# Layer-norm scales taken ahead of the last tile, routing mixed with hidden products, and a second cross attention written out with its last steps one tile later

## The reference

```python
x = x + L0_xattn(layernorm(x), ctx)      # 16 heads
x = x + L0_attn(layernorm(x))            # state space: gates, decays
x = x + L0_ffn(layernorm(x))             # 16 blocks, the best 4 of each row
x = x + L1_xattn(layernorm(x), ctx)      # one head
x = x + L1_attn(layernorm(x))            # causal self attention
x = x + L1_ffn(layernorm(x))             # 4-bit weights, quantized activations
```

## Time and profile before

| what | value |
|---|---|
| median of 3 runs | 1695.85 us (1692.62 to 1696.95) |
| the profiled execution | 1692.85 us, span of its instructions 1691.1 us |
| PE busy | 1557.8 us, 92% of the span |
| DVE / ACT / POOL busy | 1180.3 / 888.4 / 723.6 us |
| mean granted PE clock | 0.969 of full |
| PE busy, 850 to 990 us | 122.38 of 140.00, clock 0.98 |
| PE busy, 990 to 1211 us | 211.32 of 221.00, clock 0.93 |
| PE busy, 1248 to 1386 us | 124.24 of 138.00, clock 0.99 |
| PE busy, 1386 to 1442 us | 51.94 of 56.00, clock 0.97 |
| PE busy, 1442 to 1691 us | 199.20 of 249.10, clock 0.91 |

### The profile page before, as it was taken

One profiled execution on the slowest core, in us unless ns is written; L12 is line 12 of the kernel. 1 busy time (PEld: TensorE's weight loads), 2 busy tenths in 40 slices (PEclk: granted clock), 3 DMA queues, 4 the chain that ended last, 5 costly groups with the idle time before them and its releaser, 6 DMA issues. The chain is left out here.

```text
span 1691.1 us, 33888 instructions
## 1 busy us (share of the span) xinstructions
PE 1557.8 (92%) x13881; PEld 815.0 (48%) x13990; DVE 1180.3 (70%) x1952; ACT 888.4 (53%) x1189; POOL 723.6 (43%) x348
## 2 busy tenths in 40 slices
PE   6999999999999999999888989999889989799469
PEld 3445555555555555555444564344534444444124
DVE  6588888888888888887557458998622233526981
ACT  1487777777777777777463224431212222326650
POOL 1478888888787888886306813320000000000000
PEclk9999999999999999999999979999899999999779
DMA  4489999999999999999925653569779934000001
GB/s 140 128 182 192 190 192 194 186 198 188 194 193 198 195 182 198 191 190 171 185 70 156 225 226 79 143 175 209 233 311 398 393 143 188 1 1 0 1 0 50
DMA packets 555526, 282.73 MB, mean 167 GB/s; under 512 B 481760, under 2 KB 533472, under 8 KB 552304
## 3 DMA queue, kind: packets, MB, share of 16 engines
q1 hardware_dynamic: 555376, 280.63, 70.0%
HBM read 138.74 MB, written 22.54 MB: 95 GB/s over the span
## 5 line engine op out<-in xcount | busy, mean ns | idle before, releaser
L572 POOL TENSOR_TENSOR x<-x_prob,x 128x1604 bf16<-128x1604 f32 x120 | 388.1, 3234 | 143.3 <-ACT x L737 143.3
L867 DVE TENSOR_REDUCE x_negmax<-x_score 128x1 f32<-128x1604 f32 x128 | 233.6, 1825 | 17.3 <-PE x_score L613 7.2
L727 ACT ACTIVATE x_prob<-x_score,x_negmax 128x1604 f32<-128x1604 f32 x128 | 204.8, 1600 | 25.4 <-DVE x_negmax L867 20.7
L596 PE MATMUL x_ring<-x_ctx_hi,wk_split 128*128 128x400 bf16 (+1 forms) x1024 | 216.2, 333 | 0.3 <-DVE x_kT L795 0.3
L596 PE MATMUL x_ring<-wv_split,x_ctx_hi 128*128 128x512 bf16 (+1 forms) x770 | 200.3, 379 | 9.7 <-issue 7.3
L795 DVE SCALAR_TENSOR_TENSOR x_kT<-x_ring,bk,x_kT 128x400 bf16<-128x400 f32 (+1 forms) x256 | 162.2, 634 | 31.8 <-ACT x_kT L716 23.8
L737 ACT CAST x<-x_prob 128x1604 bf16<-128x1604 f32 x120 | 183.0, 1525 | 0.0
L801 DVE TENSOR_TENSOR x_v<-x_ring,x_v 128x512 bf16<-128x512 f32 (+1 forms) x208 | 143.7, 691 | 52.8 <-ACT x_v L720 50.0
L716 ACT ACTIVATE x_kT<-x_ring,bk 128x400 bf16<-128x400 f32 (+1 forms) x196 | 116.4, 594 | 91.2 <-PE x_ring L596 90.3
L720 ACT CAST x_v<-x_ring 128x512 bf16<-128x512 f32 (+1 forms) x148 | 86.5, 585 | 96.9 <-PE x_ring L596 96.9
L596 PEld LDWEIGHTS x_ring<-x_ctx_hi,wk_split 128*128 128x128 bf16 x1024 | 93.8, 97 | 87.0 <-issue 19.8
(11 more groups left out here) (347 smaller groups left out, 2399.9 us busy)
## 6 DMA issues: line engine op xcount, KB each, us to landing
y_ctx<-in_ctx SPq DMA_DIRECT2D x16, 1664.0 KB, 10.5
y_ctxT<-in_ctxT SPq DMA_DIRECT2D x16, 1601.0 KB, 13.7
x_stage<-in_ctxT SPq DMA_DIRECT2D x48, 400.0 KB, 4.4
x_q_rows<-q_rows SPq DMA_DIRECT2D x64, 128.0 KB, 3.1
m_xT<-in_L_ffn_w SPq DMA_DIRECT2D x16, 512.0 KB, 4.5
ffn_w_parts<-m_xT SPq DMA_DIRECT2D x32, 256.0 KB, 2.7
x_stage<-in_ctxT SPq DMA_DIRECT2D x16, 401.0 KB, 4.9
f_w<-ffn_w_parts SPq DMA_DIRECT2D x4, 1024.0 KB, 8.6
```

What stands on the lines that cost most here:

```text
L572: pool.tensor_tensor(ph[:, g % 2, 1, 0:NKP], prob[:, g % 2, :], ph[:, g % 2, 0, 0:NKP], ALU.subtract).then_inc(pl_done, 1)
L596: last = pe.matmul(out_, lhs, rhs, start=(i == 0), stop=(i == len(steps) - 1))
L727: nc.scalar.activation(prob[:, g % 2, :].rearrange("p (c n) -> p c n", n=QW), scores, ACT.Exp, bias=nmax[:, g % 2:g % 2 + 1], accum_out=rs ...
L867: dve.tensor_reduce(nmax[:, pair % 2:pair % 2 + 1], scores, mybir.AxisListType.XY, ALU.max, negate=True).then_inc(max_done, 1)
```

## The change

Four things are altered; what the matmuls compute is not.

1. **Scales of seven tiles ahead.** `norm_scales` computes mean, variance, `rstd` and `shift` of tiles 0 to 6 on DVE alone, at the end of the stage before, ahead of the addition of tile 7. The root is formed with a bit-level first guess and three Newton steps: 7 `BN_AGGR` and 13 small instructions, each waiting for the one before. The next block's norm begins with the normed tiles; tile 7's scales follow as `last_scales_on_vector` (1 `BN_AGGR` and the same 13) after the first four. ACT's square root is gone, and seven of its table loads with it.
2. **Block FFN.** On PE, `hidden(0)`, `hidden(1)` and `hidden(2)` stand between the routes of tiles 4 to 7; ACT's and DVE's streams follow.
3. **Second cross attention.** Steps are written out; `qs` is gone. The transposes of `o`, ACT's copy, the product `wb` and DVE's addition of tile `u - 2` stand in step `u`, behind its scores; there is a ninth step with these alone. `o` is turned into the free half of the bank of `pv`.
4. `cT` has three buffers: the third is loaded at the stage's opening, the others one tile earlier than before.

```diff
+    def norm_scales(self, dve, first, last, step, base):
+        ve, r, u = self.meanvar[:, first:last, 1], self.rstd[:, first:last, 0], self.shift[:, first:last]
+        if base:
+            dve.wait_ge(step, base)
+        for t in range(first, last):
+            dve.bn_aggr(self.meanvar[:, t, :], self.stats[:, t, :]).then_inc(step, 1)
+        done = base + last - first
+        dve.wait_ge(step, done)
+        dve.tensor_scalar(ve, ve, EPS, None, ALU.add).then_inc(step, 1)
+        dve.wait_ge(step, done + 1)
+        dve.tensor_scalar(r.bitcast(I32), ve.bitcast(I32), 1, None, ALU.logical_shift_right).then_inc(step, 1)
+        dve.wait_ge(step, done + 2)
+        dve.tensor_scalar(r.bitcast(I32), r.bitcast(I32), -1.0, ROOT_SEED, ALU.mult, ALU.add).then_inc(step, 1)
+        done += 3
+        for _ in range(3):
+            dve.wait_ge(step, done)
+            dve.scalar_tensor_tensor(u, r, -0.5, r, ALU.mult, ALU.mult).then_inc(step, 1)
+            dve.wait_ge(step, done + 1)
+            dve.tensor_tensor(u, u, ve, ALU.mult).then_inc(step, 1)
+            dve.wait_ge(step, done + 2)
+            dve.scalar_tensor_tensor(r, u, 1.5, r, ALU.add, ALU.mult).then_inc(step, 1)
+            done += 3
+        dve.wait_ge(step, done)
+        dve.scalar_tensor_tensor(u, self.meanvar[:, first:last, 0], -1.0, r, ALU.mult, ALU.mult).then_inc(step, 1)
...
     def on_vector(self, dve):
-        self.small_on_vector(dve)
-        dve.scalar_tensor_tensor(self.shift[:], self.meanvar[:, :, 0], -1.0, self.rstd[:, :, 0], ALU.mult,
-                                 ALU.mult).then_inc(self.s_shift, 1)
         self.hat_on_vector(dve, range(self.HALF))
+        self.last_scales_on_vector(dve)
         for t in self.BY_VECTOR:
...
             for t in range(NT):
+                if t == NT - 1:
+                    k.norm_scales(dve, 0, NT - 1, s_stats, NT - 1)
                 dve.wait_ge(s_o, t + 1)
...
-            for n in range(AHEAD - 1):
-                hidden(n)
+            hidden(0)
+            norm.turn_on_tensor(pe, 6)
+            routed(4)
+            hidden(1)
+            norm.turn_on_tensor(pe, 7)
+            routed(5)
+            routed(6)
+            hidden(2)
+            routed(7)
             turned_masks(0)
...
+NCT = 3
...
-        cT = k.sb(ctx, "y_ctxT", [P, 2, 2, KC, NK])
+        cT = k.sb(ctx, "y_ctxT", [P, NCT, 2, KC, NK])
...
+            def load_turned(u):
+                sp.wait_ge(s_s, u - NCT + 1)
+                for h in range(2):
+                    sp.dma_start(cT[:, u % NCT, h], ctxT[:, 2 * u + h]).then_inc(cT_in[u % NCT], 16)
+
+            def load_rows(u):
+                sp.wait_ge(s_pv, u - 1)
+                for h in range(2):
+                    sp.dma_start(cn[:, u % 2, h].rearrange("p t c -> p (t c)"), d["ctx"][2 * u + h]).then_inc(cn_in[u % 2], 16)
...
+            for u in range(2, NT):
+                if u + 1 < NT:
+                    load_turned(u + 1)
+                load_rows(u)
...
+            for u in range(NT + 2):
+                do(u, u % 2, u < NT, 1 <= u <= NT, u >= 2)
...
+                if finish:
+                    pe.wait_ge(s_o, u - 1)
+                    for j in range(KC):
+                        last = pe.transpose(pv[:, CD + P * j:CD + P * j + P], o[:, P * j:P * j + P], ident[:])
+                    last.then_inc(s_to, 1)
                 if products:
...
                     turn(0)
                     turn(1)
+                if finish:
+                    pe.wait_ge(s_w, 16)
+                    pe.wait_ge(s_of, u - 1)
+                    if u > 2:
+                        pe.wait_ge(s_x, u - 2)
+                    for j in range(KC):
+                        last = pe.matmul(wb[:], oT[:, P * j:P * j + P], wv[:, j, :], start=(j == 0), stop=(j == KC - 1))
+                    last.then_inc(s_wo, 1)
```

More of the change, by code:

```diff
@@ L105, in __init__ @@
         self.loaded = loaded
+        self.k = k
         if home is None:
[L108 to L111, removed]
+            self.meanvar, self.rstd = k.meanvar, k.rstd
         else:
@@ L178, in root_on_scalar @@
     def root_on_scalar(self, nc, act):
+        if not self.loaded:
+            return
         act.wait_ge(self.s_var, 1)
@@ L187, in turned_on_scalar, with low_on_vector @@
         last.then_inc(self.s_xT, 1)
-    def low_on_vector(self, dve):
-        for t in range(NT):
+    def low_on_vector(self, dve, tiles):
+        for t in tiles:
             c = slice(t * P, (t + 1) * P)
@@ L1380, in _ @@
             pe.wait_ge(s_in, 80)
-            for t in range(NT):
-                if t + 2 < NT:
-                    norm.turn_on_tensor(pe, t + 2)
+            for t in range(NT // 2):
+                norm.turn_on_tensor(pe, t + 2)
                 routed(t)
@@ L1494, in _ @@
             norm.on_vector(dve)
-            norm.low_on_vector(dve)
+            norm.low_on_vector(dve, range(NT // 2))
             dve.wait_ge(s_in, 80)
@@ L1557, in _ @@
             compared(0)
+            norm.low_on_vector(dve, range(NT // 2, 6))
             below(0)
@@ L1560, in _ @@
             beating(0)
+            norm.low_on_vector(dve, range(6, NT))
             masked_of(0)
@@ L1712, in cross1_batches @@
         s_w = k.sem(ctx, "y_w_in")
-        qs_in = [k.sem(ctx, f"y_qs_in{n}") for n in range(2)]
         s_s = k.sem(ctx, "y_scores_done")
@@ L1745, in _, with tile @@
             sp.wait_ge(s_w, 16)
         def each_tile(eng, do):
-            do(0, 0, True, False)
-            do(1, 1, True, True)
-            with eng.Fori(0, (NT - 2) // 2) as i:
-                for a in range(2):
-                    do(2 * i + 2 + a, a, True, True)
-            do(NT, NT % 2, False, True)
+            for u in range(NT + 2):
+                do(u, u % 2, u < NT, 1 <= u <= NT, u >= 2)
         @block.tensor
         def _(pe):
-            def tile(u, par, scores, products):
+            def tile(u, par, scores, products, finish):
+                other = 1 - par
@@ new lines, in product @@
+                def product(j):
+                    pe.wait_ge(s_tf, 4 * (u - 1) + j + 1)
+                    for i, (k0, kw) in enumerate(TGROUPS[j]):
+                        for s in range(2):
+                            last = pe.matmul(pv[L * s:L * s + L, 0:CD], pT[0:kw, j, P * i + L * s:P * i + L * s + L],
+                                             cn[0:kw, other, s, 4 * j + i, :],
+                                             start=(j == 0 and i == 0), stop=(j == NTG - 1))
+                    return last
```

183 lines of the change are left out of this document (78 added, 105 removed).

## The result

The changed kernel takes 1679.3 us (median of 6 runs, 1676.2 to 1684.8); the kernel before takes 1693.5 on the same chip. The ratio is 0.9922, 95% interval 0.9907 to 0.9937: faster by 13 us. I had predicted 1688, 8 us under the 1695.85 that I had for the kernel before, and the range 1683 to 1694, so the direction was right and the size too small. The profiled execution of the changed kernel takes 1682.2 us (span 1680.5).

The account below looks back on a forecast made before the run. PE, busy 92%, bounds the kernel. +7.2 and +0.15 against -9.0, -2.3 and -2.6 give -6.5 us: 1686.3 from the profiled execution, 1689.4 from the median; predicted 1688, range 1683 to 1694.

Parts of the forecast that it names:

- The tile of the second cross attention: Second cross attention: most PE idle inside tiles goes, 9.0 us gained, a tile takes 16.0 instead of 17.37.
- The loads: Second cross attention: a tile's loads take 16.35 us, 0.35 more than its work; slack covers the backlog, costed at nothing.
- rival 4: Second cross attention: loads bound it; at 350 GB/s 14 us more than forecast, 1702; chance 0.04.
- The opening: Opening of the second cross attention: first product 7.0 us after the start instead of 9.3, gain 2.3, between 0 and 2.6.
- The hardware loop: Second cross attention: removing the loop costed at nothing, since written-out and looped steps show no other PE idle time.
- The chain: DVE scales at stage ends: steps 0.20 us apart, 3.2 us for seven tiles; exposed parts together +7.2 us.
- rival 3: DVE's scale chain costs more per step: the median at 0.30 us, 1703.6 at twice 0.20; chance 0.07.
- The openings of state space, block FFN and self attention: At these three openings PE's first work waits for loads, so the earlier normed tile gives nothing back.
- rival 1: Openings of state space, block FFN, self attention and the FFN's end free: another 7 us, 1681; chance 0.10.
- Block FFN: Block FFN: early hidden products raise the half clock after 3.5 us; PE gains 3.8, the stage's end 2.6.
- rival 2: Block FFN: the half clock stays or comes back, the 2.6 us are gone, 1690.6; chance 0.15.
- Quantized FFN: Quantized FFN's opening: DVE's first maximum 4.8 us after the block's start instead of 4.65, a loss of 0.15.

Follow-up runs that it names:

- experiment 2: Changed kernel, second cross attention still written out with three buffers, but turns of `o`, copy, product and addition back in the tile's own step: 1694.9 us, ratio 1.0005.
- experiment 3: Changed kernel with the value-weights product moved ahead of the eight transposes of the probabilities, bringing back two of three PE stops per tile: 1688.7 us, ratio 0.9957.
- experiment 4: Changed kernel with two buffers of turned context instead of three, SP issuing the turned context in the old order: 1699.7 us, ratio 1.0034.
- experiments 9: Changed kernel, early seven-tile scales only at ends of block FFN and second cross attention, plus 30 filler matmuls before the second tile's scores: 1674.3 us, ratio 0.9883.
- experiment 10: Changed kernel with 30 filler matmuls on PE before the second tile's scores in the second cross attention as only edit: ratio 0.9922.
- Experiment 7: Changed kernel without early scales: DVE forms all eight tiles' scales in one chain at each of the five openings: 1676.5 us, ratio 0.9904.

## Why the prediction was wrong

- **The tile of the second cross attention** is the step that failed: "11.0 - 2.0 = 9.0 us gained, and a tile takes 16.0". The mechanism was right (the idle times that went are the ones named, 9.0 of them), the size was off: a tile takes 15.3, and 13.7 us were gained. I took PE's cost of a wait to be the idle in the row. The measured cost is 0.15 to 0.23 us more for each stop (experiments 2 and 3). 20 stops are gone (7, 6 and 7); at the 0.23 of the kernel before they make the 4.7 us from 9.0 to 13.7, at 0.15 they would make 3.0. (0.3 of the 4.7 is the clock in the second tile's scores, 7.03 us instead of 7.32.) Why two stops cost less each than three is open. I could have seen the overlap in the trace of before: the scores of the earlier trace rows end at 1308.16 and the next row, shown above, starts at 1308.09.
- **The loads** followed, as forecast, and "`cn` has over 20 us from its issue to its use and `cT` 32" is true of the changed kernel. What I had not seen is how much hangs on it: with two buffers in the old order the same PE steps wait for `y_ctxT` and lose all (experiment 4). That kernel is slower than the one before, at 1700, close to my rival 4, though its DMAs moved 402 to 418 GB/s around the first wait: the load was issued late, behind a stretch in which they moved nothing. I had read the 358 GB/s for a core in the Trainium skill (DMA: Bandwidth & Descriptors, Bandwidth) as a rule against the change. The same section gives that figure for both cores of an HBM domain streaming, and 425 GB/s for a 16 MB load of a core alone. This kernel runs on one core, and the trace agrees with the latter: 409 to 422 were moved and no row of PE waited for a load of the context.
- **The opening** gained 2.7 (forecast 2.3, bounds 0 and 2.6).
- **The hardware loop** "is costed at nothing": right (experiment 2). But the reason given, that steps 0 and 1 show no other idle time of PE, was misread: ahead of the second tile's scores PE stood still for 4.12 us in the kernel before, waiting for ACT's `y_prob`. The wait is there after the change too (4.11), so the sum did not suffer; experiments 9 and 10 work on it.
- **The chain**: spacing 0.20, 3.1 us; rival 3 is out. Self attention +3.0 against +3.3. First cross attention: 853.1 in the mean of seven profiles with the chain, 850.1 of five without, +3.0 against +2.5, though each group spreads over 3 to 4 us. State space: forecast +1.2. DVE's wait of 2.02 is gone at its end, as forecast, but the stage's length doesn't show it: 139.2 in the mean of five profiles with the chain, without the two in which the clock fell, and 139.2 of five without it. Second cross attention: tile 7 waited for the chain's end, 0.1.
- **The openings of state space, block FFN and self attention** get next to nothing back: 0.1 and 0.2 us where the first products could be timed, and the waits for the loads grew, as forecast. Experiment 7, without the early scales, is not slower. Rival 1 is out.
- **Block FFN**: PE gained 3.9 to the masks (forecast 3.8), the stage 3.2 to 3.3 (forecast 2.6). The clock rose 3.2 to 5 us after the first hidden product in five profiles (3.5 was taken), so each run differs by a part of that; rival 2 is out.
- **Quantized FFN**: +1.0 in the two profiles (forecast +0.15) and no step of the opening explains it (the first hidden product starts 15.65 after the block, 15.88 before). By the mean of seven profiles it is 249.3 with early scales, and it is 248.8 and 251.1 in the two with the old chain. I leave it as spread.
- **From profile to median**: the sum of the differences is -10.6 in the two profiled executions, and -13 by the ratio of all runs. The changed kernel's profiled run was 2.9 above its median. So of the 8.7 us from 1688 to 1679.3, 4.1 are the sum (the tiles' 4.7, less 0.6 in the other terms together), and 4.6 are not of the mechanism: 2.9 for that run, and 1.7 because I put 1688 above the sum's 1686.3. With the tile at its right size I would have said 1683.3, at the range's edge and still 4 us high. A sum made against a single profiled run has this uncertainty, and my range of some 5 us to each side had to hold it together with the sizes.

## What to carry to other kernels

Price a stop of PE by the starts of the rows around it, not by the idle time shown: in the stretch that ran through here, rows overlapped by about 0.17 us, and each stop lost that too. When a step gets shorter, check how far ahead of its use each load is issued, in the order of the issuing queue: here a load behind another one's wait cost PE 4.2 us of waiting and then 2.7 of lower clock, three times. Work put ahead of a stage's last tile costs its full length where the engine does not wait there, and buys only what the next stage's loads leave free; decide it place by place, and not all at once.

## What the hardware showed beside

A PE wait of 4 us in the middle of dense work brought half clock for a part of the next product: 8.2 us instead of 5.6 three times (experiment 4, mean clock 0.68), 7.0 to 8.6 us in the second tile of all ten kernels without filler. Filler matmuls of 3.45 us kept the clock at 1.00 (5.66 us). In two of twelve profiles the clock fell to 0.50 in the state space too, behind waits of up to 1.37 and 1.29 us, and the stage was some 4 and 10 us longer. Small DVE instructions on integers are 0.17 us long and 0.20 apart, as those on floats.
